# A convolution block with windowed attention: a loop round of 48 steps instead of 24, and a fixed place for the head of TensorE's loop

## What is computed

```python
x = x + conv(group_norm(x))     # 16 groups: two image columns each, all rows and channels; no learned scale

# conv(v): windowed attention
q, k, v = v @ Wq, v @ Wk, v @ Wv                 # 224 x 224 each
# each of 64 positions in an 8 x 8 window attends over the 16 windows, 8 heads of 28
sim = einsum('bmhid,bmhjd->bmhij', q * scale, k) + pos_emb
out = softmax(sim) @ v
return out @ Wo + bo
```

## Time and profile before

| | us |
|---|---|
| median of 3 runs | 3689.78 |
| lowest, highest | 3684.65, 3693.11 |
| the profiled execution | 3689.51 |
| its span, first to last instruction | 3687.7 |
| TensorE busy | 3608.1 (98%) |
| VectorE busy | 3033.8 (82%) |
| ScalarE busy | 2947.5 (80%) |
| GpSimd busy | 2053.2 (56%) |

### The profile page before, as it was taken

The page is one execution under the profiler, slowest core; times in us unless marked ns, Lnnn a source line. Parts: engine busy times, 40 slices in busy tenths (PEclk is TensorE's granted clock), DMA queues, the critical chain, the costliest instruction groups (busy, mean ns, idle before and its releaser), DMA issues.

```text
span 3687.7 us, 169098 instructions
## 1 busy us (share of the span) xinstructions
PE 3608.1 (98%) x68610; PEld 2630.1 (71%) x68610; DVE 3033.8 (82%) x5027; ACT 2947.5 (80%) x5377; POOL 2053.2 (56%) x3335
## 2 busy tenths in 40 slices
PE   6999999999999999999999999999999999999998
PEld 4777777777777777777777777777777777777776
DVE  6888888888888888888888888888888888888876
ACT  7888887888788878888888888888888888888874
POOL 5555555555555555555555555555555555555553
PEclk9999999999999999999999999999999999999999
DMA  4555555555555555555555555555555555555544
GB/s 105 142 141 147 140 138 138 148 138 141 136 151 137 141 135 151 138 141 136 145 142 142 136 147 141 141 136 146 140 142 136 144 141 144 135 145 141 144 123 118
DMA packets 255586, 513.98 MB, mean 139 GB/s; under 512 B 66352, under 2 KB 66800, under 8 KB 254992
## 3 DMA queue, kind: packets, MB, share of 16 engines
q1 hardware_dynamic: 253456, 504.35, 52.5%
q10 hardware_dynamic: 1536, 0.07, 0.0%
HBM read 118.31 MB, written 117.44 MB: 64 GB/s over the span
## 4 chain that ended last, share of the span: by engine, by line
PE 80%; issue 8%; POOL 5%; DVE 3%; ACT 2%; SPq 1%; DMA 0%; POOLq 0%; DVEq 0%; ACTq 0%
PE ps_out L343 17%; PE ps_q L343 15%; PE ps_k L343 15%; PE ps_v L343 13%; PE ps_o L386 12%; PE ps_s L374 9%; ACT xn L508 2%; POOL xlo L784 1%; POOL sc L773 1%; POOL newton L755 1%; DVE part L670 1%; POOL sc L794 1%; DVE sc L699 1%; DVE pt_f L712 1%; DVE x_sb L682 0%
## 5 line engine op out<-in xcount | busy, mean ns | idle before, releaser
L773 POOL TENSOR_TENSOR sc<-sc,mx 128x512 f32<-128x512 f32 x512 | 537.4, 1050 | 890.7 <-DVE mx L706 890.7
L508 ACT ACTIVATE xn<-x_sb,norm_add,norm_mul 112x128 f32<-112x128 f32 x2048 | 1018.9, 601 | 2.0 <-issue 2.0
L694 DVE TENSOR_TENSOR olo<-ps_o,ohi 128x512 f16<-128x512 f32 x512 | 354.1, 692 | 529.3 <-ACT ohi L565 519.4
L794 POOL TENSOR_TENSOR sc<-sc,rs 128x512 f32<-128x512 f32 x512 | 537.2, 1049 | 429.0 <-DVE rs L726 428.4
L343 PE MATMUL ps_out<-ohi,wo_s 128*112 128x256 f16 x4096 | 722.4, 279 | 1.9 <-DVE x_sb L682 1.8
L343 PE MATMUL ps_q<-xhi,wqk 112*128 112x512 f16 x2048 | 611.2, 380 | 35.1 <-issue 32.2
L550 ACT ACTIVATE sc<-sc 128x512 f32<-128x512 f32 x512 | 324.0, 633 | 402.3 <-POOL sc L773 402.2
L343 PE MATMUL ps_k<-xhi,wqk 112*128 112x512 f16 x2048 | 609.7, 379 | 1.5 <-ACT k_cut L557 0.8
L343 PE MATMUL ps_v<-wv_s,xhi 112*128 112x224 f16 x4096 | 560.4, 259 | 0.0
L386 PE MATMUL ps_o<-p_bd,v_sb 128*32 128x128 f32 x16384 | 553.7, 276 | 6.9 <-DMA p_bd<-pt_f 6.3
L784 POOL TENSOR_TENSOR xlo<-xn,xhi 112x1024 f16<-112x1024 f32 x256 | 547.3, 2138 | 14.9 <-ACT xhi L531 14.9
(11 more groups left out here) (78 smaller groups left out, 5836.6 us busy)
## 6 DMA issues: line engine op xcount, KB each, us to landing
k_bd<-k_cut SPq DMA_DIRECT2D x1024, 128.0 KB
p_bd<-pt_f SPq DMA_DIRECT2D x2048, 64.0 KB, 2.3
x_sb<-in_x SPq DMA_DIRECT2D x256, 448.0 KB, 4.5
out_y<-x_sb SPq DMA_DIRECT2D x254, 448.0 KB, 3.5
out_y<-x_sb SPq DMA_DIRECT2D x8, 112.0 KB, 2.5
k_cut<-in_L_conv_Wq SPq DMA_DIRECT2D x2, 98.0 KB
k_cut<-in_L_conv_Wk SPq DMA_DIRECT2D x2, 98.0 KB
k_cut<-in_L_conv_Wv SPq DMA_DIRECT2D x2, 98.0 KB
```

What stands on the lines that cost most here:

```text
L508: nc.scalar.activation(xn[:, b % 2, :, c4, :, :, nw].rearrange("p r c q -> p q r c"), x_sb[:, b % XBUFS].rearrange("p ch (nh r w) -> p (ch ...
L694: nc.vector.tensor_tensor(olo[:, g % 2], in_x_order(ps_o[:, :]), ohi[:, g % 2], ALU.subtract).then_inc(o_lo, 1)
L773: nc.gpsimd.tensor_tensor(rows, rows, mx[:, t % 2].unsqueeze(2).broadcast_to(by_row), ALU.subtract).then_inc(shifted, 1)
L794: nc.gpsimd.tensor_tensor(rows, rows, rs[:, t % 2].unsqueeze(2).broadcast_to(by_row), ALU.mult).then_inc(probs, 1)
```

## The change

The round of the loop becomes 48 steps, two turns of the six image buffers. ROUND_BUFS = 2 is the number of turns, IMAGES = 12 the number of images in a round. What was counted per round with XBUFS images is now counted with IMAGES; the semaphores of each image buffer, which move once per turn, move twice per round. ROUNDS becomes 10. The steps, their order and the buffers are the same. For TensorE alone the loop gets `head_slot` = 104: its first instruction is loaded 104 instruction slots into a block of fetched instructions. The code ahead is padded to that place, and the padding is jumped over once.

```diff
+ROUND_BUFS = 2
+IMAGES = ROUND_BUFS * XBUFS
-PERIOD = 4 * XBUFS
+PERIOD = 4 * IMAGES
...
-        def rounds(eng, step, **prepare):
+        def rounds(eng, step, head_slot=None, **prepare):
...
-            with nc.Fori(0, ROUNDS, engines=[eng.engine], hint_back_edge=True) as i:
+            with nc.Fori(0, ROUNDS, engines=[eng.engine], hint_back_edge=True, head_slot=head_slot) as i:
...
-                wait(sp, y_stored[ch][b % XBUFS], 16 * (b // XBUFS), i, 16)
+                wait(sp, y_stored[ch][b % XBUFS], 16 * (b // XBUFS), i, 16 * ROUND_BUFS)
...
-                             else x[bass.ds(b + i * XBUFS, 1), c].rearrange("o p y z -> p (o y z)")
+                             else x[bass.ds(b + i * IMAGES, 1), c].rearrange("o p y z -> p (o y z)")
...
-                    wait(pe, stats, STAT_OPS * (b - 1) + 1, i, STAT_OPS * XBUFS)
+                    wait(pe, stats, STAT_OPS * (b - 1) + 1, i, STAT_OPS * IMAGES)
...
-            rounds(pe, step, before_11=bound_weights, before_4=weights_split, before_0=out_weights_split)
+            rounds(pe, step, {pe.engine: HEAD_SLOT}, before_11=bound_weights, before_4=weights_split, before_0=out_weights_split)
...
+HEAD_SLOT = 104
```

More of the change, by code:

```diff
@@ L257, in load_x @@
                 c = slice(ch * CP, ch * CP + CP)
-                wait(sp, y_stored[ch][b % XBUFS], 16 * (b // XBUFS), i, 16)
+                wait(sp, y_stored[ch][b % XBUFS], 16 * (b // XBUFS), i, 16 * ROUND_BUFS)
                 sp.dma_start(x_sb[:, b % XBUFS, ch],
-                             x[b + i * XBUFS, c].rearrange("p y z -> p (y z)") if isinstance(i, int)
-                             else x[bass.ds(b + i * XBUFS, 1), c].rearrange("o p y z -> p (o y z)")
+                             x[b + i * IMAGES, c].rearrange("p y z -> p (y z)") if isinstance(i, int)
+                             else x[bass.ds(b + i * IMAGES, 1), c].rearrange("o p y z -> p (o y z)")
                              ).then_inc(x_loaded[ch][b % XBUFS], 16)
@@ L268, in store_y @@
                 per_step(sp, final, 4 * b + 3, i)
-                sp.dma_start(out[b + i * XBUFS, c].rearrange("p y z -> p (y z)") if isinstance(i, int)
-                             else out[bass.ds(b + i * XBUFS, 1), c].rearrange("o p y z -> p (o y z)"),
+                sp.dma_start(out[b + i * IMAGES, c].rearrange("p y z -> p (y z)") if isinstance(i, int)
+                             else out[bass.ds(b + i * IMAGES, 1), c].rearrange("o p y z -> p (o y z)"),
                              x_sb[:, b % XBUFS, ch]).then_inc(y_stored[ch][b % XBUFS], 16)
@@ L483, in square @@
                     return
-                wait(act, x_loaded[ch][b % XBUFS], 16 * (b // XBUFS + 1), i, 16)
-                wait(act, summed, 2 * CH * (b - 1) + CH + ch + 1, i, 2 * CH * XBUFS)
+                wait(act, x_loaded[ch][b % XBUFS], 16 * (b // XBUFS + 1), i, 16 * ROUND_BUFS)
+                wait(act, summed, 2 * CH * (b - 1) + CH + ch + 1, i, 2 * CH * IMAGES)
                 nc.scalar.activation(sq[:, ch, :], x_sb[:, b % XBUFS, ch], ACT.Square).then_inc(squared, 1)
@@ L492, in add_bias @@
                 per_image(act, normed, b, i, G)
-                wait(act, summed, 2 * CH * b + CH, i, 2 * CH * XBUFS)
+                wait(act, summed, 2 * CH * b + CH, i, 2 * CH * IMAGES)
                 nc.scalar.activation(x_sb[:, b % XBUFS, ch], x_sb[:, b % XBUFS, ch], ACT.Identity,
@@ L637, in stat_op @@
                 mean, msq = st[:, 0:G], st[:, G:2 * G]
-                wait(dve, stats, STAT_OPS * b + n, i, STAT_OPS * XBUFS)
+                wait(dve, stats, STAT_OPS * b + n, i, STAT_OPS * IMAGES)
                 if n == 0:
@@ L659, in group_sums @@
                     return
-                wait(dve, x_loaded[ch][b % XBUFS], 16 * (b // XBUFS + 1), i, 16)
+                wait(dve, x_loaded[ch][b % XBUFS], 16 * (b // XBUFS + 1), i, 16 * ROUND_BUFS)
                 if ch == 0:
@@ L668, in group_squares @@
                     return
-                wait(dve, squared, CH * b + ch + 1, i, CH * XBUFS)
+                wait(dve, squared, CH * b + ch + 1, i, CH * IMAGES)
                 nc.vector.tensor_reduce(part[:, b % 2, ch, G:2 * G], sq[:, ch].rearrange(by_group, g=G, w=WW // G),
@@ L753, in root @@
                         (rstd, y, newton[:, :], ALU.mult))):
-                    wait(pool, refined, ROOT_OPS * b + 4 * k + n, i, ROOT_OPS * XBUFS)
+                    wait(pool, refined, ROOT_OPS * b + 4 * k + n, i, ROOT_OPS * IMAGES)
                     nc.gpsimd.tensor_tensor(out_[:, :], left, right, op).then_inc(refined, 1)
@@ L761, in norm_factors @@
                 per_image(pool, normed, b - 2, i, G)
-                wait(pool, factors_ready, 2 * b, i, 2 * XBUFS)
+                wait(pool, factors_ready, 2 * b, i, 2 * IMAGES)
                 nc.gpsimd.tensor_tensor(norm_mul[:, b % 2], rstd[:, :], plus_scale[:, :], ALU.mult).then_inc(factors_ready, 1)
```

## The result

| | before | changed |
|---|---|---|
| median, us (6 runs each) | 3692.76 | 3661.39 |
| lowest, highest | 3684.65, 3695.7 | 3659.29, 3664.97 |
| the profiled execution | 3689.51 | 3659.29 |
| its span | 3687.7 | 3657.5 |

The ratio is 0.9919, 95% interval 0.9906 to 0.9931: the changed kernel is 0.8% faster, by 31 us. The forecast was 3666 us, in a range of 3657 to 3680. (One detail of the description above is off by one: TensorE projects q, k and v of step t+4, not t+5. No number hangs on it.)

What follows compares the result with a forecast made beforehand. TensorE, busy 98% of the span, was taken to bound the kernel, idle 1.59 us at each of 19 loop edges behind its branch. 3689.5 - 16.5 - 9.0 + 1.5 + 0 = 3665.5, so 3666 us; range 3657 to 3680.

Steps and rivals of the forecast that it cites:

- the block at 469.2: TensorE's instruction packet at a loop edge, inferred to be requested some 1.2 us earlier, on entering the branch's block.
- Part 1: TensorE's loop edges: taken jumps fall from 19 to 9, ten edges at 1.65 us each, 16.5 us gone.
- part 2: TensorE's loop head at slot 104: target requested 1.0 us earlier at each of nine edges, 9 us gone.
- rival 1: TensorE's loop edges: the slot does nothing and nine edges keep 1.6 us, giving 3674.5 us; chance 0.20.
- rival 1b: TensorE's loop edges: all of the idle time goes, giving 3660 us; chance 0.12.
- Part 3: Entering the loop: the jump over the padding may have to fetch its target, costing 0 to 1.6 us, taken as 1.5.
- Part 4: The other engines' doubled loop bodies: taken as costing 0; bounds 0 and 18 us with a stall of 4.1 us on VectorE.
- Nothing is late in their place: In the loop TensorE waits for no other engine; the others have 1.2 us to spare in each 7 us step.

Runs made afterwards that it cites:

- the series of slots: Changed kernel (48 steps a round) with HEAD_SLOT 0, 56 and 152 instead of 104: 3675.57, 3672.65 and 3662.08 us.

## Why the prediction was right, and where it was not

**What bounds the kernel** was read rightly: 19 idle stretches of TensorE, its own branch, no other engine. That the block at 469.2 was asked for before the branch, at the entry of the branch's block, was an inference then; the series of slots, the packets of q8 that move with the slot, and the kernel without a hint bear it out.

**Part 1, 16.5 us for ten edges**, has the price of an edge right: (3405.1 - 3373.0) / 19 = 1.69 us by the windows, where 1.65 was taken. But it holds only together with part 2. As a term of its own it is wrong: the doubling alone changed nothing, because it moved the branch from a slot of some 92 to 112 to one near 26, where a late branch costs its idle time and the clock behind it. (If the head of the kernel before is at h, its branch is at h + 178 and that of the doubled loop at h + 92, modulo 256. The doubled loop's 3,556 ns at edges belongs to a slot near 26, which makes h about 190; the 2,965 ns of the kernel before belong to a slot near 92, which makes it about 170. The two agree to some 20 slots, and both lie inside the 168 to 208 of the prediction. The body counts 13,149 instructions, five fewer than predicted, so the changed kernel's branch stands at slot 196, not 201.) The prediction's rival 1, "the slot does nothing and nine edges keep 1.6 us", put that case at 3674.5 without asking where an unpinned head would leave the branch.

**Part 2, 9 us, was too small.** The request came earlier by more than the 1.0 us taken: the branch fell by 1.8 us, just above the upper end of the 1.0 to 1.7 worked out, and all of the idle time went, 1.59 to 0.03 us. The failed steps are the choice of the lower end and the even 14 ns per instruction. At nine edges the idle time fell by 14.3 - 0.3 = 14.0 us, 5 more than the term. This was rival 1b, 3660, given 0.12, and as idle time it is what happened. In time the term was off by less: the 0.5 us that each edge still costs took 4.6 us of it back, which leaves 9 x (1.69 - 0.51) = 10.6 us.

**Part 3, 1.5 us**: one idle stretch of 0.8 us at the entry, and 1.0 us until the loop's first ps_q.

**Part 4, nothing**: right in time, for the reason given (each engine has a hint, and slow issue leaves it time). q14's packets are there. The rule of the Trainium skill, Runtime: NRT & Kernel Launch, section "Instruction fetch mechanics", that most engines have room for 512 instructions, agrees with the trace: bodies of about 420 stay, and with bodies of up to some 830 the packets come all through the loop. Its other half, that a taken branch to a block outside stalls, came true on these engines only without the hints.

**"Nothing is late in their place"** failed: ps_tot waits for `both`, 1.8 us seen as idle time, and by the windows an edge still costs 0.5 us, 4.6 in all. The 1.2 us that VectorE has to spare per step are an average; in the chain at 474 to 476 us, around the group sums, it had none.

**Sum.** By idle time the terms give 3689.5 - 16.5 - 14.0 + 0.8 = 3659.8, and the profiled execution took 3659.3, but this match is luck in part. The loop gave 27.5 us (16.9 + 10.6), not 30.5; the entry cost 1.0; and 3.7 us came from behind the loop, where no term put anything. There the kernel before was granted 0.97 of the clock and the changed one 0.99. Whether this belongs to the change is open: the kernels with 24 steps a round and head slots 16 and 104 take 151 us behind these steps as the kernel before does, those with 48 steps 146 to 151. The sum of 3665.5 was 6.2 us too long: 3.7 from behind the loop, 1.6 from part 2, 0.4 and 0.5 from parts 1 and 3.

## What to carry to other kernels

Where an engine's loop body is larger than what its sequencer holds, the time of the jump depends on where the closing branch stands in its block of 256 instructions: early in the block the target is asked for too late (slots 26 to 148 here), in the last few slots the exit from the loop pays (244 and 250). Any edit to the code ahead of the loop or inside it moves that place, so an unrolling or a small edit can gain or lose 0.6% for no reason of its own, as the two kernels with 24 steps did here; fix the place first, then compare. And read the idle time of the engine behind a branch, not the branch's own duration.

## What the runs showed of the hardware that I had not expected

- Some idle times of 2.2 us and more at an edge, between stretches of full work, were followed by a stretch at the lower clock (0.57 granted in 4 us); those of 1.6 us in the loop of the profiled kernel before were not. In the doubling alone this added 11 us to 20 us of idle time. Idle time of 2.4 us at its first edge was not followed by it, and the kernel without the other engines' hints, with two shorter waits at an edge, was granted 0.66 in 1157 to 1167 us.
- Leaving a loop whose branch stood at slot 250 cost 3.00 us of idle time; at 244 it was 1.9 us; at 196 none.
- With the branch at slot 196 and a hint one packet came, 1.2 us ahead of the branch; without the hint one came 1.4 us ahead and another 1.1 us behind its start.
- An unhinted branch on TensorE shows its wait in the branch (3,961 ns), one on VectorE behind it (63 ns and then 3.14 us idle).
- 20.7 packets of 8 KB came on q14 for each round of 48 steps (197 in 9.5 rounds), while TensorE's come as 16 KB: the other engines are fed in smaller blocks.
